# A perceiver block on one core: one activation table set for exponentials and logarithms, decays ahead of the tangents, and ten weight turns moved from the attention to the tail

## The reference

```
x = x + attention(LN(x), ctx, ctx, mask)      # softmax(q k^T / sqrt(8) + mask) v, then Wo

u = LN(x)                                     # state space layer
raw = u @ Wp.T + bp ; delta_raw, b_raw, c_raw = split(raw, 3)
delta = softplus(delta_raw + delta_bias) ; alpha = softplus(alpha_log)
a = min(exp(-delta * alpha), 1 - 1e-4) ; b = tanh(b_raw) ; c = tanh(c_raw)
p = a*a + c*c ; r = b*b ; q = a*b
disc = (p - r)**2 + 4*q*q
scale = max(sqrt(0.5 * (p + r + sqrt(disc + EPS)) + EPS), 1)
a, b, c = a/scale, b/scale, c/scale
bu = b * exp(log_gamma) * (u @ W_in_n.T)      # W_in and W_out divided by their largest singular value if over 1
state = scan(a, bu) over time ; y_hat[t] = c[t] * state[t-1]
x = x + y_hat @ W_out_n.T

h = gelu(LN(x) @ bin(w1).T + b1)              # bin(w) = mean(|w|) of a row * sign(w)
x = x + h @ bin(w2).T + b2
```

## Time and profile before

| | |
|---|---|
| median of three runs | 278.73 us |
| profiled execution | 274.99 us, of which 273.2 us from first to last instruction (the span) |
| busy share | TensorE 90%, VectorE 81%, ScalarE 76%, GpSimd 37% |
| chain of waits by engine | TensorE 60%, VectorE 17%, DMA 7%, issue 6%, ScalarE 4% |
| granted TensorE clock, whole span | 0.975 |
| units | to 228.7 us; tail from there to 273.2 us |

### The profile page before, as it was taken

One profiled execution on the slowest core, in us unless ns is written; L12 is line 12 of the kernel. 1 busy time (PEld: TensorE's weight loads), 2 busy tenths in 40 slices (PEclk: granted clock), 3 DMA queues, 4 the chain that ended last, 5 costly groups with the idle time before them and its releaser, 6 DMA issues.

```text
span 273.2 us, 11667 instructions
## 1 busy us (share of the span) xinstructions
PE 245.4 (90%) x4911; PEld 182.1 (67%) x4911; DVE 221.6 (81%) x407; ACT 207.5 (76%) x441; POOL 101.2 (37%) x225
## 2 busy tenths in 40 slices
PE   8799879998999999999999999999999986822875
PEld 7476456776777667677777777777776755612764
DVE  6876899887888999888999898999989921649961
ACT  3675469888898979899898989898897885398032
POOL 6467786643444333334444444412211120200310
PEclk9999999999999999999999999999999998985999
DMA  7896945888442424253433422232222000000001
GB/s 224 316 318 182 294 143 161 246 196 271 132 127 73 127 70 133 79 154 72 154 114 87 128 71 79 72 102 85 83 71 72 2 4 2 1 0 0 2 0 41
DMA packets 21088, 30.66 MB, mean 112 GB/s; under 512 B 4272, under 2 KB 15052, under 8 KB 20908
## 3 DMA queue, kind: packets, MB, share of 16 engines
q1 hardware_dynamic: 17708, 28.00, 33.8%
q0 software_dynamic: 624, 1.06, 1.4%
q10 hardware_dynamic: 2704, 0.85, 1.2%
HBM read 22.43 MB, written 7.47 MB: 109 GB/s over the span
## 4 chain that ended last, share of the span: by engine, by line
PE 60%; DVE 17%; DMA 7%; issue 6%; ACT 4%; SPq 2%; POOL 2%; ACTq 0%; POOLq 0%; DVEq 0%
PE ps L509 20%; PE ps L492 13%; PE ps L468 11%; PE ps L363 10%; DVE pmax L1339 6%; PE ps L358 3%; DMA k_rows<-k_parts_dram 2%; DMA ctx_buf<-in_ctx_dram 2%; SPq L246 1%; DMA x_sb<-in_x_dram 1%; DMA k_parts_dram<-k_parts 1%; DVE k_parts L1528 1%; ACT probs L901 1%; SPq L248 1%; PE ps L796 1%
## 5 line engine op out<-in xcount | busy, mean ns | idle before, releaser
L1339 DVE TENSOR_REDUCE pmax<-ps 128x2 f32<-128x1024 f32 x128 | 155.1, 1222 | 17.3 <-PE ps L468 15.3
L901 ACT ACTIVATE probs<-ps 128x512 f32<-128x512 f32 x256 | 138.8, 596 | 8.5 <-PE ps L492 5.3
L492 PE MATMUL ps<-q_max,k_rows 59*128 59x128 bf16 x1024 | 84.5, 218 | 0.6 <-issue 0.4
L509 PE MATMUL ps<-probs,v_all 128*9 128x128 f32 x2048 | 80.0, 274 | 1.4 <-ACT probs L901 0.9
L468 PE MATMUL ps<-k_rows,q_all 56*128 56x512 bf16 x256 | 79.3, 382 | 0.8 <-DVE pmax L1339 0.3
L492 PEld LDWEIGHTS ps<-q_max,k_rows 59*128 59x128 bf16 x1024 | 54.2, 94 | 10.3 <-ACT probs L901 8.1
L509 PEld LDWEIGHTS ps<-probs,v_all 128*9 128x9 f32 x2048 | 43.2, 90 | 15.7 <-ACT probs L901 2.1
L1148 POOL CAST max_cols<-negmax 128x2 bf16<-128x2 f32 x32 | 6.2, 192 | 106.8 <-DVE negmax L1345 106.8
L468 PEld LDWEIGHTS ps<-k_rows,q_all 56*128 56x128 bf16 x256 | 23.1, 93 | 24.8 <-issue 20.8
L352 PE MATMUL ps<-ones 128*128 128x128 f32 x76 | 12.6, 336 | 11.1 <-ACT k_parts L1037 10.1
L352 PEld LDWEIGHTS ps<-ones 128*128 128x128 f32 x76 | 12.0, 250 | 11.5 <-ACT k_parts L1037 10.5
(11 more groups left out here) (186 smaller groups left out, 324.6 us busy)
## 6 DMA issues: line engine op xcount, KB each, us to landing
k_rows<-k_parts_dram SPq DMA_DIRECT2D x59, 192.0 KB
k_parts_dram<-k_parts SPq DMA_DIRECT2D x16, 384.0 KB, 3.8
ctx_buf<-in_ctx_dram SPq DMA_DIRECT2D x16, 256.0 KB, 5.6
k_rows<-k_parts_dram SPq DMA_DIRECT2D x59, 32.0 KB
mask_sb<-in_mask_1x1xSxS_ff_dram SPq DMA_DIRECT2D x1, 1024.0 KB, 7.2
q_all<-q_rows_dram SPq DMA_DIRECT2D x2, 336.0 KB
k_rows<-k_parts_dram POOLq DMA_DIRECT2D x3, 192.0 KB, 3.9
q_rows_dram<-q_parts SPq DMA_DIRECT2D x2, 288.0 KB, 3.7
```

Of the source, the lines that this page charges most:

```text
L492: t = pe.matmul(dst, k_rows[rows, i % 4, at:at + P], q_max[rows, i % 2, :], start=not masked, stop=True, skip_group_check=masked)
L509: t = pe.matmul(ps[at:at + HEAD_COLS, 6, 0:P], v_all[:, KT * (i // PAIRS) + 4 * c + j, first + HEAD_COLS * h: first + HEAD_COLS * h + HEAD ...
L901: act.activation(probs[:, u % CHUNKS, h, :], ps[:, key_bank(u, h), :], ACT.Exp).then_inc(probs_ready, 1)
L1339: dve.tensor_reduce(pmax[:, i % 2, :, c], ps[:, bank:bank + 2, :], AX.X, ALU.max).then_inc(pmax_ready, 1)
```

## The change

Four edits.

1. ScalarE's program names the table set that has both exp and ln, behind its first DMA issue. The compiler then loads that set there and none for the logarithms.
2. In the gates each half runs |raw delta|, exp and ln in a row, the logarithm of alpha moves ahead to where alpha's exponential is, and the decay's exponentials move ahead of both tanh of c. VectorE's two steps on alpha move ahead of max(delta, 0).
3. The turns of W_in and W_out (two) and of binarised w1 and w2 (eight) leave the units' bank 7 for `finish`, behind the product with Wo, in banks 3, 0 and 4, and so do their three copies on ScalarE. W_o and the three of Wp are turned together in round 0, the vectors alone in round 1, nothing in rounds 3 and 4. At `at` 7 of rounds 3 and 4 `sum_norms` waits for the side bank to be taken (as round 2 did) in place of the copy.
4. The products of ones before the second norm are two instead of eight.

```diff
-    WARM_LN2, WARM_Y, WARM_Y0 = 8, 11, 12
+    WARM_LN2, WARM_Y, WARM_Y0 = 2, 11, 12
...
-                elif at == 6 and m in (0, 1, 3, 4):
+                elif at == 6 and m < 2:
                     side_taken(i)
                     if m == 0:
                         pe.wait_ge(ld["w"], 32)
-                        turn_weights(0, 4)
-                    elif m == 1:
+                        turn_weights(7, W_O, 4)
+                    else:
                         turn_vectors()
-                        turn_weights(4, 2)
-                    else:
-                        turn_binary(m - 3)
                 elif at == 7 and k + SQ_PERIOD < SQUARINGS:
                     if m < 2:
                         pe.wait_ge(once("wT_ready"), m + 1)
-                    elif m > 2:
-                        pe.wait_ge(once("wT_ready"), m)
                     else:
                         side_taken(i)
                     sum_norms(m + 1)
...
                     by_token(h, PROJ, xnT, wT[:, W_O, :], once("attn_done"))
+                turn_weights(3, W_IN, 2)
+                turn_binary(0, 0)
+                turn_binary(4, 1)
                 keep_busy(TURN, WARM_LN2)
...
                 for h in range(2):
+                    pe.wait_ge(once("wT_ready"), 5 if h else 3)
                     pe.wait_ge(once("lnT_ready"), h + 1)
...
             act.dma_start(ident[:, :], ident_in).then_inc(ld["ident"], 16)
+            act.preload_act_table_set("natural_log_exp_and_others")
...
                 elif at == 6 and m == 0:
                     act.wait_ge(once("w_turned"), 1)
-                    copy(wT[:, 0:4, :].rearrange("p a d -> p (a d)"), ps[:, 7, :], once("wT_ready"))
+                    copy(wT[:, W_O:, :].rearrange("p a d -> p (a d)"), ps[:, 7, :], once("wT_ready"))
                 elif at == 6 and m == 1:
                     act.wait_ge(once("w_turned"), 2)
-                    copy(wT[:, 4:6, :].rearrange("p a d -> p (a d)"), ps[:, 7, 0:2 * P], once("vec_ready"))
                     copy(vec[:, 2:VECS], ps[:, 7, 3 * P + 2:3 * P + VECS], once("wT_ready"))
-                elif at == 6 and m == 3:
-                    act.wait_ge(once("w_turned"), 3)
-                    copy(w1T[:, :, :].rearrange("p a d -> p (a d)"), ps[:, 7, :], once("wT_ready"))
-                elif at == 6 and m == 4:
-                    act.wait_ge(once("w_turned"), 4)
-                    copy(w2T[:, :, :].rearrange("p a d -> p (a d)"), ps[:, 7, :], once("wT_ready"))
...
             act.activation(sv[:, 1:2], sv[:, 0:1], ACT.Exp, scale=-1.0).then_inc(once("alpha_step"), 1)
+            act.wait_ge(once("alpha_step"), 3)
+            act.activation(sv[:, 2:3], sv[:, 1:2], ACT.Ln, bias=1.0).then_inc(once("alpha_step"), 1)
...
+            for dst, src in ((wT[:, 0:W_O, :], ps[:, 3, 0:2 * P]), (w1T[:, :, :], ps[:, 0, :]), (w2T[:, :, :], ps[:, 4, :])):
+                act.wait_ge(once("w_turned"), 5)
+                copy(dst.rearrange("p a d -> p (a d)"), src, once("wT_ready"))
...
-            act.wait_ge(once("alpha_step"), 3)
-            act.activation(sv[:, 2:3], sv[:, 1:2], ACT.Ln, bias=1.0).then_inc(once("alpha_step"), 1)
-            for h in range(2):
                 act.wait_ge(once("exp_ready"), h + 1)
                 act.activation(SP_LN[:, cols(h)], SP_EXP[:, cols(h)], ACT.Ln, bias=1.0).then_inc(once("sp_ln_ready"), 1)
+
+            act.wait_ge(once("small_ready"), 2)
+            for h in range(2):
+                act.wait_ge(once("delta_ready"), h + 1)
+                act.activation(G_A0[:, cols(h)], DELTA[:, cols(h)], ACT.Exp, scale=sv[:, 4:5]
+                               ).then_inc(once("a0_ready"), 1)
...
             for h in range(2):
                 gate_tanh(h, 1)
-            act.wait_ge(once("small_ready"), 2)
-            for h in range(2):
-                act.wait_ge(once("delta_ready"), h + 1)
-                act.activation(G_A0[:, cols(h)], DELTA[:, cols(h)], ACT.Exp, scale=sv[:, 4:5]
-                               ).then_inc(once("a0_ready"), 1)
...
-            each("own", lambda h, t: dve.tensor_scalar(DELTA[:, t], bank(h, RAW_DELTA)[:, 0:HALF], sv[:, 5:6], 0.0,
-                                                       ALU.add, ALU.max), "abs_ready")
             dve.wait_ge(once("alpha_step"), 4)
...
             dve.tensor_scalar(sv[:, 4:5], sv[:, 6:7], -1.0, None, ALU.mult).then_inc(once("small_ready"), 1)
+            each("own", lambda h, t: dve.tensor_scalar(DELTA[:, t], bank(h, RAW_DELTA)[:, 0:HALF], sv[:, 5:6], 0.0,
+                                                       ALU.add, ALU.max), "abs_ready")
```

More of the change, by code:

```diff
@@ L588, in turn_vectors, with turn_weights, turn_binary @@
                 pe.wait_ge(ld["vec"], 16 * 5)
-                pe.transpose(ps[:, 7, 3 * P:3 * P + VECS], vec_nat[:, :], ident[0:VECS, 0:VECS])
-            def turn_weights(first, n):
+                pe.transpose(ps[:, 7, 3 * P:3 * P + VECS], vec_nat[:, :], ident[0:VECS, 0:VECS]
+                             ).then_inc(once("w_turned"), 1)
+            def turn_weights(bank, first, n):
                 for i in range(n):
-                    t = turn(ps[:, 7, P * i:P * i + P], w_nat[:, first + i, :])
+                    t = turn(ps[:, bank, P * i:P * i + P], w_nat[:, first + i, :])
                 t.then_inc(once("w_turned"), 1)
-            def turn_binary(half):
+            def turn_binary(bank, half):
                 pe.wait_ge(once("w_bin_ready"), 2)
                 for i in range(HB):
-                    t = turn(ps[:, 7, P * i:P * i + P], w_bin[:, HB * half + i, :])
+                    t = turn(ps[:, bank, P * i:P * i + P], w_bin[:, HB * half + i, :])
                 t.then_inc(once("w_turned"), 1)
```

## The result

| | before | changed |
|---|---|---|
| median of 20 runs each | 277.11 us | 275.17 us |
| profiled execution, span | 273.2 us | 271.8 us |
| first product with v starts (unit 0) | 34.80 us | 36.89 us |
| unit 0 to unit 64 | 100.32 us | 99.64 us |
| unit 64 to unit 127 | 92.50 us | 91.47 us |

The ratio is 0.9931 with a 95% interval of [0.9903, 0.9959]: 1.9 us faster, between 1.1 and 2.7. The difference that was forecast, 2.0 us, is inside the interval. The three runs of before that the forecast started from had a median of 278.73; over 20 runs it is 277.11.

The account below looks back on a forecast made before the run. Bounds: ScalarE's DMA queue at the start, TensorE and VectorE by turns in the units, serial waits in the tail. Gates -1.64, tail turns 0, units -0.4, start 0: -2.0 us from 278.73, said as 276.8 us, range 275.6 to 279.3.

Parts of the forecast that it names:

- The difference: Whole kernel: gates, tail turns, units and start together make the profiled execution 2.0 us shorter.
- The base: Whole time: median of the runs shown, 278.73 us, 3.74 above the profiled 274.99, an offset carried over unchanged.
- drift between measurements: Whole time: with C's upper part, gives 0.13 chance of being slower by over 0.5%.
- The gates: Tail's gates: one table load goes, larger gain behind tanh; 1.64 us shorter, bounds 1.3 to 1.8.
- rival D: Gates: chain does not shrink, VectorE's serial ops or the root's load are late; gain under 0.8, total 277.6 us; 9%.
- The units: 128 units: two seams losing four turns give 0.2 us each, 0.4 in all, bounds -0.1 and 0.6.
- other reading: Units: less TensorE work did not shorten a seam, VectorE's norms were late instead; lower bound -0.03 us a seam.
- Ten turns in the tail: Before the second norm: ten turns and three copies replace six products of ones; cost 0, with 0.2 us of cover.
- The start: ScalarE's DMA queue: table load behind the first issue does not hold back the others; cost 0, bounds 0 and 1.28 us.
- B: Start: table load holds the issue queue, x issued 1.28 us later; total 278.0 us; 15%.
- C: Start: as B, and x lands late among the mask's 1 MB; 2.8 to 4.3 us lost, total 279.5 to 281; 9%.
- A: Second norm: TensorE's clock stays low through it, |x| 0.5 us later, total 277.3 us; 24%.

Follow-up runs that it names:

- e3: Kernel before with only the turns and copies moved to the tail and products of ones cut from eight to two: 276.52 us, ratio 0.9974.
- e4: Kernel before with only the table set named behind the first DMA issue, old order of gates: 275.60 us, ratio 0.9926.
- e1: The changed kernel measured again with no edit: 274.02 us, ratio 0.9885 to before.
- e6: Changed kernel with GpSimd's steps on the binarised weights in pairs 21, 23, 25 and 27 instead of 20 to 23: 273.22 us, ratio 0.9887 to before.
- e12: Kernel before with only GpSimd's steps on the binarised weights moved from pairs 20 to 23 to pairs 15 to 18: 278.29 us, ratio 1.0056.
- e9: Changed kernel with the table set named behind all six of ScalarE's DMA issues instead of the first: 274.72 us, ratio 0.9937 to before.
- e2: Kernel before with only the table set named and the gates reordered; turns and eight products of ones kept: 275.96 us, ratio 0.9948.
- e5: Kernel before with only the gates reordered and no table set named: 280.44 us, ratio 1.0111.

## Why the prediction was right or wrong

**The base is the step that failed.** "The median of the runs shown is 278.73, 3.74 above that; I carry the difference over unchanged: 276.7, and say 276.8." The time forecast is the median of three runs less 2.0 us. The 20 runs of before have a median of 277.11, so the base was 1.6 us too high; from 277.11 the same 2.0 us give 275.1, against 275.17 measured. The three runs ranged over 1.1 us, all 20 over 5.3 (274.02 to 279.34), and they are three of the four longest of the 20. That is rare by chance alone, and why they were so long is open. The profiled execution, 274.99 us and so 3.2 below the shortest of the three, was the sign that the three did not span the kernel's times; the prediction took the 3.74 for a fixed offset. It names a drift between measurements, for the slower side only, and the range has no term for it on the faster side.

The largest part of the spread that the profiles show lies ahead of the first product with v, which begins 34.80 to 39.56 us into them. The landing of x varies by 1.6 us. The chain of waits goes on through a load of the context (`ctx_buf`) that took 5.99 us in before, 6.59 in the changed kernel's first profile and 7.00 in e3. TensorE's clock in the tail adds 1 us in some profiles.

**The difference: right, in part by luck.** 2.0 us were forecast, and 1.9 (1.1 to 2.7) and 3.2 (1.8 to 4.6) measured. By the profiles the two terms add up to 2.5 us, less what the turns cost in the tail (up to 0.2): the gates stood in the sum with 0.2 us too much and the units with 0.6 too little, and the run times can't tell 2.0 from 2.5.

**The gates: right in place, 1.45 instead of 1.64 us.** One load went, p - r and the root followed as worked out, and the root kept up (first root at 247.48, sum at 248.05), so rival D falls. The forecast put tanh 0.3 us nearer to |x|, and it came 0.15 nearer; that is most of the 0.2 us missing, and the total is within the bounds of 1.3 to 1.8. The place was right, "the larger gain is behind tanh" (1.30 us of it), but the reason was wrong, as it gave that gain to the new order. e4 gets 1.42 us with no reordering. I had worked out the new order alone, and not what the load's removal gives with the old one.

**The units: mis-sized, 0.4 instead of 1.0 us.** The stretch without turns, 6.34 us, was taken for the floor, less the 0.31 of the slowed sum of squares: 6.03. The floor is 5.87 (changed kernel, e1, e3, e6), and the two seams gave 0.44 each, all that four turns cost at 0.11 a turn. The row had another 0.15 us in it that the prediction did not see. Behind the same two copies of `power`, ScalarE starts the next exponential 0.66 us after the first of them in before (173.09, 173.75) and 0.51 in the changed kernel (174.50, 175.01). This 0.15 us went from round 2's seam as well, in every kernel with the turns moved, and stayed in every one without, e12 included. What held the exponential is open. That VectorE's sum held rounds 1 and 2 was right: e6 shows 5.87 with the slow sum gone, where they had 6.19. The prediction's other reading, that VectorE sets the seams even where four turns stand, falls with e3 (5.88 without the turns).

**Ten turns in the tail: 0 as predicted, to within 0.2 us** (e3 against e12, e6 against e4). The cover was smaller than the 0.2 us worked out. In the changed kernel's first profile TensorE's clock was at 0.50 until 235.0, the last of the ten turns was done at 235.2 instead of 234.5, and the copies ended at 236.57 instead of 235.96. That made xnT's copy 0.3 us late and the first |raw delta| up to 0.2. One small sum does not come out of its rows: four turns in 1.02 and in 0.66 us differ by 0.09 a turn, not 0.12.

**The start: 0, as predicted, as far as the profiles tell.** B and C fall by the issue times: with the load at 1.21 to 2.49 us the first x is issued at 2.04, as without it. e9 shows no gain from the later load, though one of 0.6 us could hide in its times. The evidence used, that an issue ran ahead of a copy, held for a table load.

**A, the clock,** came in part. The ten turns did run at the low clock, 2.27 us for A's 2.3, and the last copy ended at 236.57 for A's 236.75; but the clock was at 1.00 from 235.0, ahead of the second norm's turn and products, so that A's 0.5 us did not follow. In other profiles it was low in those products, and not because of the turns: with full eight products of ones and no turns, e2 had it at 0.50 there, and copy to abs 8.51 us. It fell in some profiles and not in others of equal tails. And it cost most, 1.07 us, in a place that the prediction did not name, the MLP's first hidden products.

## What to carry to other kernels

Before crediting a reordering with a gain, work out what the removed cost gives with the old order: here one named table set gave all of the gates' 1.4 us, and the same order without the name cost 3.4. Where two engines alternate as the limit, a stretch that happens to lack the work is a floor only after what else is different in it has been taken off; GpSimd's neighbour op hid 0.3 us here, and a late exponential another 0.15. And a difference of a few parts in a thousand has to be forecast as a difference: a median of three runs, with a spread of 2% between executions, is no base for a range of 1.3%. Where the profiled execution lies far from the few runs at hand, that is a sign of the spread and not an offset to carry over.

## What the runs showed of the hardware

- A table load took 1.28 us in all fourteen profiles. In the tail it started 0.02 us after the activation ahead of it and the next one 0.01 to 0.02 us after it. DMA issues behind it in ScalarE's stream went out while it ran (load 1.21 to 2.49 us, x issued at 2.04).
- The compiler's choice of sets, without a name: exp and ln in turn made it change the set at each of them, five loads in the gates of e5.
- VectorE's sum of squares over 128x128 took 0.28 us alone. Where one of GpSimd's elementwise steps over 128x512 was under way at its start it ended 0.14 to 0.15 us after that step: it took 0.60 us in the changed kernel (170.38 to 170.98, the step ending at 170.83), and 1.35 in e12 (147.33 to 148.68, the step ending at 148.53). VectorE's row maxima and copies kept their usual times beside the same steps.
- TensorE's clock fell to 0.50 in the middle of the MLP in five of fourteen profiles, and that made the same products take 3.2 to 3.45 instead of 1.89 us.
